# A recurrent layer on eight cores: hi and lo halves of streamed weights loaded and multiplied apart, and four filler groups pumped earlier

## The reference

```
xi, z = split(x @ Win.T)                                   # fp32
lam = exp(-8 * softplus(omega) * sigmoid(xi @ Wl.T + bl))
v   = xi @ Wv.T + bv
h_t = lam_t * (h - 2 v_t (v_t.h)/(v_t.v_t)) + (1 - lam_t) * xi_t   # scan over t
a   = (silu(z) * h) @ Wout.T
x   = layernorm(x + a)
x   = layernorm(x + quantized(x) @ (ternary - 1).T * scale + bias)
```

## Time and profile before

| | us |
|---|---|
| median of the 2 timed runs | 4276.12 |
| lowest, highest | 4204.22, 4348.01 |
| the profiled execution | 4174.64 |
| its slowest core (5), first to last instruction | 4173.1 |
| TensorE matmul busy there | 3266.9 (78%) |
| VectorE, ScalarE busy | 1234.1, 562.0 |

### The profile page before, as it was taken

One profiled execution on the slowest core, in us unless ns is written; L12 is line 12 of the kernel. 1 busy time (PEld: TensorE's weight loads), 2 busy tenths in 40 slices (PEclk: granted clock), 3 DMA queues, 4 the chain that ended last, 5 costly groups with the idle time before them and its releaser, 6 DMA issues.

```text
span 4173.1 us, 52517 instructions; the slowest of 8 cores (4136.1 to 4173.1 us)
## 1 busy us (share of the span) xinstructions
PE 3266.9 (78%) x20764; PEld 2556.2 (61%) x20764; DVE 1234.1 (30%) x2310; ACT 562.0 (13%) x1454; POOL 128.1 (3%) x124
## 2 busy tenths in 40 slices
PE   4855257754898879888898889887997899888965
PEld 3643246621687657765786568764886578656852
DVE  1011412312243133331153134233143215213443
ACT  0101000100121122011121022112201112102210
POOL 0011010000000000000000000000000000000000
PEclk9977678976899989987999989998999999999977
DMA  4444242233452444324442445234533444244502
GB/s 134 146 153 149 81 161 92 86 108 117 147 198 61 126 150 179 106 83 145 172 172 75 136 154 188 89 113 148 182 122 86 156 174 171 71 140 153 192 31 81
DMA packets 139109, 545.23 MB, mean 131 GB/s; under 512 B 16499, under 2 KB 25076, under 8 KB 106100
## 3 DMA queue, kind: packets, MB, share of 16 engines
q1 hardware_dynamic: 131188, 516.70, 36.9%
q0 software_dynamic: 5376, 16.78, 1.2%
q10 hardware_dynamic: 2304, 8.39, 0.5%
HBM read 491.48 MB, written 50.33 MB: 130 GB/s over the span
## 4 chain that ended last, share of the span: by engine, by line
PE 55%; DMA 21%; DVE 12%; issue 5%; ACT 4%; POOL 2%; SPq 1%; DVEq 0%; ACTq 0%; POOLq 0%
PE pb L152 53%; DMA WLV<-wls 4%; DMA WLV<-wvs 3%; DMA WIN<-w_in 3%; DMA WOU<-wos 2%; DMA WLV<-w_l 1%; DMA WOU<-w_out 1%; DMA WLV<-w_v 1%; DMA R<-w_v 1%; DMA R<-w_l 1%; SPq L157 1%; DVE XFM L725 1%; DMA Y<-w_out 1%; DMA WIN<-w_ffn 1%; PE pb L682 1%
## 5 line engine op out<-in xcount | busy, mean ns | idle before, releaser
L152 PE MATMUL pb<-XI,WLV 128*128 128x256 bf16 x11520 | 1324.1, 278 | 181.0 <-DMA WLV<-wls 45.7
L152 PEld LDWEIGHTS pb<-XI,WLV 128*128 128x128 bf16 x11520 | 1141.7, 100 | 363.2 <-issue 206.7
L152 PE MATMUL pb<-XFM,WIN 128*128 128x256 f32 x4096 | 1007.6, 405 | 92.3 <-ACT ZS L266 50.7
L152 PEld LDWEIGHTS pb<-XFM,WIN 128*128 128x128 f32 x4096 | 817.6, 203 | 243.8 <-issue 119.2
L152 PE MATMUL pb<-WOU,LAM 128*128 128x512 bf16 x1440 | 350.7, 401 | 80.0 <-DVE WOU L809 29.9
L152 PEld LDWEIGHTS pb<-WOU,LAM 128*128 128x128 bf16 x1440 | 142.3, 101 | 276.9 <-issue 151.1
L377 DVE TENSOR_TENSOR_SCAN GC<-LAM,ZRO 128x256 f32<-128x256 f32 x128 | 88.6, 692 | 671.2 <-ACT LAM L357 658.4
L152 PE MATMUL pb<-XI,Y 128*128 128x256 bf16 x768 | 118.4, 331 | 148.5 <-DVE Y L471 79.5
L260 DVE TENSOR_TENSOR XI<-pb,XI 128x256 bf16<-128x256 f32 x128 | 53.7, 424 | 523.6 <-ACT XI L257 523.6
L152 PEld LDWEIGHTS pb<-XI,Y 128*128 128x128 bf16 x768 | 90.2, 119 | 176.7 <-issue 152.5
L893 DVE TENSOR_TENSOR R<-pb,XTM 128x512 f32<-128x512 f32 x32 | 22.1, 690 | 557.7 <-PE pb L152 554.3
(11 more groups left out here) (172 smaller groups left out, 2042.7 us busy)
## 6 DMA issues: line engine op xcount, KB each, us to landing
WIN<-w_in SPq DMA_DIRECT2D x256, 512.0 KB, 3.7
WLV<-wls SPq DMA_DIRECT2D x112, 1024.0 KB, 5.1
WLV<-wvs SPq DMA_DIRECT2D x112, 1024.0 KB, 4.9
WOU<-wos SPq DMA_DIRECT2D x224, 256.0 KB, 3.2
XFM<-x_fm POOLq DMA_DIRECT2D x64, 128.0 KB, 6.9
XTM<-x_tm POOLq DMA_DIRECT2D x16, 512.0 KB, 6.8
WLV<-w_l SPq DMA_DIRECT2D x8, 1024.0 KB, 7.8
wls<-WLV SPq DMA_DIRECT2D x16, 512.0 KB, 4.5
```

Source lines behind the costliest of these rows:

```text
L152: return e.matmul(o, l, rr, start=st, stop=sp)
```

## The change

1. In both weight phases, from tile 1 on, the load of a group is two DMAs: the hi half (512 KB, 128 rows of 4 KB) on semaphore `dl0`/`dl1`, then the lo half on `dl2`/`dl3`. Both wait for `wlv_free` as before.
2. The 48 matmuls of a group are put in three passes: wh*xi_hi, wh*xi_lo, wl*xi_hi. The first pass waits for the hi half, the third for the lo half. In tile 0 both waits are the old one.
3. `pump(3)` ahead of the first chain becomes `pump(7)`.
4. `pump(8)` behind the second `dhg` becomes `pump(4)`.

By the rule of `pump` the groups are then placed 7, 7, 2, 4, 4, 2, 1 and 5.

```diff
-                t_w = dma("sync", wslotb, d_wls[jc], "dl%d" % sl,
+                t_w = dma("sync", wslotb[:, 0:N], d_wls[jc][:, 0:N],
+                          "dl%d" % sl,
                           waits=(wlv_free[sl],) + split_done["wl"])
+                t_w2 = dma("sync", wslotb[:, N:2 * N], d_wls[jc][:, N:2 * N],
+                           "dl%d" % (sl + 2),
+                           waits=(wlv_free[sl],) + split_done["wl"])
+            if tile == 0:
+                t_w2 = t_w
...
                 mm(pb[bank][:, pcol:pcol + TT], wh, xih,
                    ic == 0 and jc % 2 == 0, False, waits=w0)
-                mm(pb[bank][:, pcol:pcol + TT], wl_, xih, False, False)
             for ic in range(NIC):
...
-                tok = mm(pb[bank][:, pcol:pcol + TT], wh, xil,
+                mm(pb[bank][:, pcol:pcol + TT], wh, xil, False, False,
+                   waits=(t_xi[NIC - 1],) if ic == 0 else ())
+            for ic in range(NIC):
+                wl_ = wslotb[:, N + ic * 128: N + (ic + 1) * 128]
+                xih = XIb[:, ic * TT:(ic + 1) * TT]
+                tok = mm(pb[bank][:, pcol:pcol + TT], wl_, xih,
                          False, ic == NIC - 1 and jc % 2 == 1,
-                         waits=(t_xi[NIC - 1],) if ic == 0 else (),
+                         waits=(t_w2,) if ic == 0 else (),
                          inc="pe" if ic == NIC - 1 else None)
...
-        pump(3)
+        pump(7)
...
-        pump(8)
+        pump(4)
```

More of the change, by code:

```diff
@@ L325, in build @@
                 wh = wslotb[:, ic * 128:(ic + 1) * 128]
-                wl_ = wslotb[:, N + ic * 128: N + (ic + 1) * 128]
                 xih = XIb[:, ic * TT:(ic + 1) * TT]
@@ L480, in build @@
                 wslotb = WLV.bitcast(BF16)[:, sl * 2 * N:(sl + 1) * 2 * N]
-                t_w = dma("sync", wslotb, d_wvs[jc], "dl%d" % sl,
+                t_w = dma("sync", wslotb[:, 0:N], d_wvs[jc][:, 0:N],
+                          "dl%d" % sl,
                           waits=(wlv_free[sl],) + split_done["wv"])
+                t_w2 = dma("sync", wslotb[:, N:2 * N], d_wvs[jc][:, N:2 * N],
+                           "dl%d" % (sl + 2),
+                           waits=(wlv_free[sl],) + split_done["wv"])
+            if tile == 0:
+                t_w2 = t_w
             bank = (jc // 2) % 4
@@ L980, in build @@
               "dxf0", "dxf1", "dxt",
-              "do", "dw0", "dw1", "dl0", "dl1", "wo0", "wo1", "wo2", "wo3"):
+              "do", "dw0", "dw1", "dl0", "dl1", "dl2", "dl3",
+              "wo0", "wo1", "wo2", "wo3"):
         sems[s] = nc.alloc_semaphore(s)
```

## The result

The changed kernel takes 4151.19 us (median of 11 runs, 4125.75 to 4286.28) against 4212.91 us (10 runs) for the kernel before. The ratio is 0.9885, with a 95% interval of 0.9847 to 0.9923: 1.15% faster, within the 2%. On a second occasion, with 12 runs beside 17 of before, it was 0.9964 (0.9917 to 1.001), which can't be told from no change. The ratios leave out executions in which a die stayed long at the 0.81 clock; medians do not.

The account below looks back on a forecast made before the run. The bound was TensorE's own work (busy 78%) plus places where its queue stands still. Regular waits -41, pump(7) +24, pump(4) with the strike -45 gave -62 from 4174.6, 4113; the time was put at 4130, range 4085 to 4185.

Parts of the forecast that it names:

- regular waits: Weight phases: TensorE waits once per pair of groups for a 1 MB load, 46 us in all; forecast -41.
- strike: POOL's x loads delay a weight load and the clock falls, 7.2 us a tile; forecast 3.5 at its new place.
- ahead of the first chain: Four more filler groups before the first chain, covering nothing: +15.6 us per tile.
- second chain: Filler left in only 2 steps, four steps bare at 2.5 us instead of 5.54: -12.2 us per tile.
- behind the second dhg: One filler group instead of five between gate and projection, 22.8 us becoming about 6.3: -16.5 us per tile.
- tile's end: Four groups moved behind group 27, +13.8 us, plus x-load delays of 0.9 for group 29 and 1.6 for 31.
- The pumps' price: Cost and return of moving filler groups: +15.6 ahead of the first chain, -12.2 second chain, -16.5 behind the second dhg.
- three signs of being wrong: Weight stretches stay at 182 us, clock falls at the tile's end, or WIN waits grow over 4 us per tile.
- The first (more is won): Rival: all regular waits and the x loads' strike go, bare chain near full clock: -102 us, 4073; chance 0.2.
- The second (the split buys nothing): Rival: the stream is short of bandwidth, the lo half waits where the whole did: -21 us, 4154; chance 0.13.
- The third (the 0.81 clock decides): Rival: denser TensorE work calls the clock limiter more often, 25.5 us an episode; about 4280 us, chance 0.07.
- The fourth (in series): Rival: the two halves of each load are served one after the other, +470 us, near 4600; chance 0.02.

Follow-up runs that it names:

- The halves alone: The changed kernel with pump(3) and pump(8) put back, keeping split loads and the new matmul order; no ratio, tile 441.3 us, weight phase 176.0.
- the pumps alone: The kernel before with pump(7) and pump(4), whole 1 MB loads and the old matmul order; no ratio, tile 451.7 us, 1.9 more than before.
- The run with x loads in the Gram stage: The changed kernel with XTM and XFM loads waiting for the last weight group; no ratio, tile 440.1 us, end 19.3, weight phase 171.7.
- two loads needed together: The kernel before with loads split, the first matmul waiting for both halves, old order and pumps; no ratio, tile 457.4 us, 7.6 slower than before.
- the densest kernel: The changed kernel with pumps at 3 and 8, x loads in the Gram stage and halved WIN blocks; no ratio, second occasion 4048.29 to 4472.9 us.

## Why the prediction came out as it did

The forecast was 4130 us, -1.5% and within 2%; it came out at 4151 us and -1.15%, and -0.36% on the second occasion. That the medians differ by 61.7 us, almost the -62 of the sum, is luck: the stretches show some 37. Per tile, the terms of the sum against the table:

| us per tile | forecast | measured | 
|---|---|---|
| weight phase (regular waits -5.9, strike -7.2 + 1.0) | -12.1 | -13.4 |
| ahead of the first chain | +15.6 | +15.5 |
| second chain | -12.2 | -12.0 |
| behind the second dhg | -16.5 | -16.0 |
| tile's end (13.8 + 0.9 + 1.6) | +16.3 | +20.0 |
| sum, with -0.4 in other stretches | -8.9 | -6.3 |

**The regular waits** went as argued: half the load in time for the first pass, the other before the third. In tile 4 of core 5 the loads of both kinds landed in (min, median, max):

```profile
DMA to landing us min/median/max: 3.7/4.6/5.5
```

The hi half has about 4.9 us from its issue, and the median of the 224 hi halves was 4.1. I had left 5 of 46 us; 9.7 us of waits in the view are left in all. The division into 46 us of regular waits and 50 of strike, read from one tile, bears up: the last tile of before, which has no XFM loads, loses 6.5 us in its phase (176.7 against 170.2), as do the regular waits of the sum, 6.6. But the two do not come off apart. The halves alone brought 7.8 us a tile, since they soften the strike as well, and moving it the other 5.6; the pumps alone brought 4.9.

**The pumps' price** was right to 0.5 us in each of three terms. Tile 0 and the last tile are not like the others, which the factor of 7 in the sum passes over: tile 0 pays for the pumps and gains nothing, and the last tile's phase gains 6.4 us and not 13.4. The step of the bare chain at clock 0.50, read in the last tile, was the same 2.68 us.

**The step that was mis-sized** is the strike: "I allow 0.9 us for group 29's load, 1.6 for 31's". In tile 3 of core 5 group 29 waited 0.47, 31 4.71, and the second fall of the clock cost 1.55 more. The end was forecast at +16.3 us a tile and measured +20.0. I had such a strike as my bound and not as my value. What I overlooked is that the place had become worse: before, two weight loads of 1 MB, issued 5.2 us apart, met the x loads; now 512 KB of WIN and 2 MB of weights were issued within 2.5 us of each other on SP's queue just as POOL issued its 2 MB. The run with x loads in the Gram stage shows it to be this term: with them gone the end is 19.3, 4.2 less, and its longest wait for WIN 1.1. Those 19.3 are 15.8 over the 3.5 of before, 13.8 for the four groups and 2.0 for ordinary waits, so nearly all of the 2.5 that I had allowed here was needed without any strike. The 1.0 for the weights was not paid: TensorE came to them late, and the phase is 170.4.

**The signs.** The phases (170.4, even under the 172 to 175), the waits for weights, the second chain and the filler ahead of the first came as the prediction had listed them. But two of its three signs of being wrong appeared as well, and both belong to this step: the clock fell at the tile's end (0.73 in the stretch above), and waits for WIN grew by 31 us over the six to seven tiles of the view, 4.4 to 5.2 a tile.

**The rivals.** The first (more is won) got its weight phase, 170.4, but not the end, and the bare chain ran mostly at low clock. The second (the split buys nothing) falls with the halves alone. The third (the 0.81 clock decides) did not decide this comparison, but it did come: in the profile after, two of the eight cores had it for more than 380 us each, and in one of the experiments' executions it lasted, for a mean of 3375 us a core. The fourth (in series) falls with the run of two loads needed together, 1.7% and not 11%.

The Trainium skill (DMA: Bandwidth & Descriptors, Rules for kernel authors) asks for at least 1 MiB per DMA. That run agrees with it in sign: two loads of 512 KB in place of one cost 0.25 us a group. The halves alone show its limit: with the second half not needed until the third pass, the same two loads leave a weight phase that is 7.8 us shorter than with the single load. The fixed cost of about 2 us that the prediction quotes is given there (Anatomy of one DMA) for loads that GpSimd issues; these are issued from SP, and no run here isolates such a cost for them.

## What to carry to other kernels

A double-buffered load that lands just after its use begins is cheaply cured by splitting it in the order of use, but only with the order of the work changed to match: each edit alone gave nothing or a loss. Before moving filler, ask what it hides; here it hid nothing in either place, so moving it cost every wait it met at the new one, and it had kept the clock up in the chain that it left: a bare step takes 2.68 us at 0.50 and 2.02 before the clock falls. And this burst of 2 MB cost 4.2 to 6.0 us a tile wherever it met a stream that was nearly bound (176.0, 175.4 and 176.4 against 170.0, 170.0 and 171.7 in the weight phase, 23.5 against 19.3 at the end): look in the DMA row for the stretch in which nothing is streamed, and put it there.

## What the runs showed of the hardware

Splitting the rows of a load from 8 KB to 4 KB made the DMA engines busier at the same rate: a share of 0.54 at 194 GB/s became 0.59 at 194 and 195, and the run with nothing but the loads split (two loads, needed together) has 0.55 at 184 (the stretch shown there), where 0.51 at 183 stood in the earlier trace rows. The page's packet counts go with it, before and after (of the slowest core of each, 5 and 7):

```profile
DMA packets 139109, 545.23 MB, mean 131 GB/s; under 512 B 16499, under 2 KB 25076, under 8 KB 106100
```

```profile
DMA packets 171368, 545.27 MB, mean 131 GB/s; under 512 B 20083, under 2 KB 28660, under 8 KB 167028
```

The clock of 0.81 is the larger unknown of this kernel. One execution of the densest kernel had it for 3375 us a core and took 4461 us, while another of its runs took 4048. On the two chips that ran the kernels with halved WIN blocks, these two kernels had more of it in their profiles (means over the cores of 493, 838 and 3375 us) than the five others run there (223 to 426 us). That fits a limiter that answers to dense work, as the Trainium skill (TensorE: Matmul & The Clock Gate, Part 1) has it, but three profiles don't show it. Against it stand the halves alone, on a third chip, with 755 us and whole WIN blocks, while the other three kernels there had 112 to 379, and ten of the eleven runs of the kernel before there, which took 4230 to 4533 us beside one of 4174. So what calls the clock, and whether the last kernels lose in it what they win in their stretches, is open.
